# Latent attention inside a three-part block: two heads' rotated rows in one product, norm and latents in one block, first scores over three pairs of banks

## What is computed

```
kv_c = x @ W_kv;  kv_c = kv_c * rsqrt(mean(kv_c^2) + eps) * g_kv      # 32 values a token
q_c  = x @ W_q                                                         # 64 values a token
k_content, v, q_content = heads of kv_c @ W_kdec, kv_c @ W_vdec, q_c @ W_qdec   # 16 heads x 8
k_rope, q_rope = rotate(x @ W_krope), rotate(q_c @ W_qrope)            # 16 heads x 32
scores = (q . k) / sqrt(40), causal;  out = softmax(scores) @ v;  x += out @ W_o
```

## Time and profile before

| what | us |
|---|---|
| median of 3 runs | 5512.19 |
| the runs | 5452.62 to 5550.69 |
| the profiled execution, its own time | 5483.86 |
| its span (first to last instruction) | 5481.7 |
| mean granted TensorE clock over the span | 0.931 of full |

### The profile page before, as it was taken

How to read it: one execution, slowest core, us unless ns; L and a number is a source line. 1 busy time by engine, 2 the same in 40 slices (tenths; PEclk the granted TensorE clock), 3 DMA queues, 4 the chain that set the end, 5 groups by cost and what they waited for, 6 DMA issues and landing times. The chain is left out here.

```text
span 5481.7 us, 143773 instructions
## 1 busy us (share of the span) xinstructions
PE 5159.2 (94%) x46548; PEld 3167.1 (58%) x46548; DVE 3782.6 (69%) x8327; ACT 3553.5 (65%) x10714; POOL 3509.2 (64%) x4464
## 2 busy tenths in 40 slices
PE   7999999999999985899999999799999999999998
PEld 4666666666666652343434443466666666666665
DVE  5888888787887851343434444588888878888785
ACT  4888888888888850022222222488888888888885
POOL 6988888888888842000000000698888888888884
PEclk9999999999999985587978998799999999999998
DMA  2121221212212101000000000212222121221211
GB/s 73 46 60 48 55 54 45 59 49 57 52 49 60 45 24 23 0 1 1 1 1 1 1 1 1 62 46 57 51 54 57 43 60 48 56 52 45 61 47 34
DMA packets 297779, 216.59 MB, mean 40 GB/s; under 512 B 83196, under 2 KB 294680, under 8 KB 296216
## 3 DMA queue, kind: packets, MB, share of 16 engines
q1 hardware_dynamic: 296984, 206.69, 14.9%
HBM read 41.87 MB, written 1.05 MB: 8 GB/s over the span
## 5 line engine op out<-in xcount | busy, mean ns | idle before, releaser
L545 POOL TENSOR_TENSOR inv<-ssm,neg_half 128x8 f32<-128x8 f32 x768 | 1361.5, 1773 | 121.2 <-DVE ssm L864 55.9
L559 POOL TENSOR_TENSOR rot<-t 128x256 f32<-128x256 f32 x1536 | 1123.9, 751 | 334.4 <-DVE t L853 265.2
L736 ACT ACTIVATE prob<-ps,nmx,inv 128x96 f32<-128x96 f32 x3072 | 1286.1, 434 | 52.4 <-DVE nmx L850 42.9
L632 PE MATMUL ps<-w_qkv,xs 128*128 128x512 f32 x1536 | 875.0, 652 | 59.7 <-issue 30.0
L1293 ACT ACTIVATE ptl<-ps_l 128x1024 f32<-128x1024 f32 (+1 forms) x288 | 281.1, 976 | 946.6 <-PE ps_l L1168 713.4
L839 DVE TENSOR_REDUCE mx<-ps 128x4 f32<-128x384 f32 x768 | 424.9, 553 | 385.8 <-PE ps L659 382.4
L736 ACT ACTIVATION_READ_ACCUMULATOR prob<-ps,nmx,inv 128x1 f32 x3072 | 632.9, 206 | 0.0
L823 DVE TENSOR_TENSOR t<-ps,tab_s 128x256 f32<-128x256 f32 x1536 | 573.8, 413 | 37.4 <-issue 30.6
L729 ACT COPY vt<-ps 128x256 f32<-128x256 f32 x768 | 285.9, 372 | 471.5 <-PE ps L670 459.4
L831 DVE TENSOR_TENSOR prob<-prob,rec 128x384 f32<-128x384 f32 x768 | 557.6, 726 | 26.3
L720 ACT ACTIVATE sq<-ps 128x512 f32<-128x512 f32 x768 | 472.1, 615 | 112.8 <-PE ps L632 112.0
(11 more groups left out here) (201 smaller groups left out, 8641.7 us busy)
## 6 DMA issues: line engine op xcount, KB each, us to landing
vs<-vt SPq DMA_DIRECT2D x768, 96.0 KB, 2.2
vs<-vt SPq DMA_DIRECT2D x768, 64.0 KB, 2.0
vs<-vt SPq DMA_DIRECT2D x768, 32.0 KB, 1.8
xs<-x_a SPq DMA_DIRECT2D x384, 32.0 KB, 1.9
w_qkv<-in_L_ffn_Wqkv SPq DMA_DIRECT2D x48, 256.0 KB, 3.8
w_qkv<-in_L_ffn_Wqkv SPq DMA_DIRECT2D x48, 128.0 KB, 2.9
w_o<-in_L_ffn_Wo SPq DMA_DIRECT2D x12, 512.0 KB, 4.4
w<-in_L_ffn_W SPq DMA_DIRECT2D x12, 341.0 KB
```

What stands on the lines that cost most here:

```text
L545: nc.gpsimd.tensor_tensor(inv[:, n % 4], ssm[:, n % 2], neg_half[:, 0:2 * HU], ALU.pow).then_inc(z["inv_ready"], 1)
L559: nc.gpsimd.tensor_tensor(rot[:, n % 4, half[w]], t1[:, n % 2, half[w]], t2[:, n % 2, half[w]], ALU.add).then_inc(z["rotated_" + w], 1)
L632: pe.matmul(ps[:, j % 2, :], xs[:, j // UT % 2, :], w_qkv[:, 0:2, u * 256:(u + 1) * 256], start=True, stop=True).then_inc(z["qk_ready"], 1)
L736: e = nc.scalar.activation(prob[:, n % 2, h, :], scores[:, h % 2, h // 2, :], ACT.Exp, scale=inv[:, n % 4, h:h + 1], bias=nmx[:, n % 2, h: ...
```

## The change

1. **Rope.** One product a group: the weights' columns of a head are its 32 plain ones and then its 32 swapped ones, so that 128 result rows hold both heads, plain and swapped. `turn` holds cos on the plain and signed sin on the swapped rows. VectorE multiplies the 128 rows by it into ra, and, since plain and swapped rows must meet on the same partitions, makes rb in two more operations of 32 partitions, one a head. GpSimd adds 32 rows of each head, two operations. The row of ones of kT is set once. The content rows of all heads are made once (qd, kd), and SP copies a pair's rows from them into qT and kT by four DMAs a pair. ScalarE clears the row for the maxima in slot 1 of each pair.
2. **Slots.** Eight ropes at t = 0, 4, ..., 28; the turn at 4 goes to 5, the sums at 6 and 24 to 7 and 25.
3. **Norm and latents** are one block: the loads start ahead of the norm, wait for no zeroing, and the latents of group n-2 run between the norm's steps for n and n-1.
4. **Ahead of the loop** only ropes 0 and 1 come first; the others stand between the S items (EARLY), and S items take banks 4, 0 and 2 in turn.

```diff
-            pe.wait_ge(z["wl_in"], WL)
-            pe.wait_ge(z["wl_zero"], WZ)
-            for n in range(G):
...
+            for n in range(G + 2):
+                if n < G:
+                    norm_mean(nc, z, pe, nb, mean_w, q0 + n, n)
+                if 1 <= n <= G:
+                    norm_var(nc, z, pe, nb, mean_w, q0 + n - 1, n - 1)
+                if n >= 2:
+                    latents(n - 2)
+                if 1 <= n <= G:
+                    norm_spread(nc, z, pe, nb, ones_w, q0 + n - 1, n - 1)
+                if n >= 2:
+                    latent_squares(n - 2)
+                    latent_spread(n - 2)
             for n in range(G):
+                pe.matmul(ps[:, 3, :], wl_qd[:, :], qc[:, cols], start=True, stop=True).then_inc(z["qd_mm"], 1)
+                pe.matmul(ps[:, 6, :], wl_kd[:, :], kvc[:, cols], start=True, stop=True).then_inc(z["kd_mm"], 1)
...
-            def rope(pair, j, half):
+            def rope(pair, j):
+                pe.matmul(ps[:, 7, :], ws[w][:, :], src, start=True, stop=True).then_inc(z["a_ready"], 1)
...
+                bank = early_bank(y) if early else 4
+                if y == 0:
+                    pe.wait_ge(z[f"qk_rows_{b}"], 64 * (twos + 1))
+                    if not isinstance(pair, int):
+                        pe.wait_ge(z["rows_cleared"], 2 * pair)
+                if not early:
                     pe.wait_ge(z["s_read"], pair * NI + y)
+                elif y >= 3:
+                    pe.wait_ge(z["s_read"], y - 2)
...
-        TURN = {4: (0, 2), 19: (0, 3), 22: (1, 0), 29: (1, 1)}
-        SUM = {6: 0, 13: 1, 24: 2}
+        TURN = {5: (0, 2), 19: (0, 3), 22: (1, 0), 29: (1, 1)}
+        SUM = {7: 0, 13: 1, 25: 2}
+        EARLY = {0: 2, 1: 3, 2: 4, 3: 5, 10: 6, 12: 7}
...
...
+            sp.wait_ge(z["qd_copied"], G)
+            sp.wait_ge(z["kd_copied"], G)
+            for pair in range(PAIRS + 1):
+                if pair >= 2:
+                    sp.wait_ge(z["t_ready"], (pair - 1) * NI)
+                for src, dst in ((qd, qT), (kd, kT)):
+                    for h in range(2):
+                        sp.dma_start(dst[64 * h + RD + 1:64 * h + QS, pair % 2, :], src[(2 * pair + h) % HEADS * CD:((2 * pair + h) % HEADS + 1) * CD, :]).then_inc(z[f"qk_rows_{pair % 2}"], 16)
...
-                nc.gpsimd.tensor_tensor(dst[:, b, n * GT:(n + 1) * GT], ra[:, j % 2, :], rb[:, j % 2, :], ALU.add).then_inc(z["roped"], 1)
+                for h in range(2):
+                    rows = slice(64 * h, 64 * h + RD)
+                    nc.gpsimd.tensor_tensor(dst[rows, b, n * GT:(n + 1) * GT], ra[rows, j % 2, :], rb[rows, j % 2, :], ALU.add).then_inc(z["roped"], 1)
+                    pool.wait_ge(z["roped"], 2 * (pair * NR + j) + h + 1)
...
+                        if t == 1:
+                            for h in range(2):
+                                row = slice(64 * h + RD, 64 * h + RD + 1)
+                                nc.scalar.activation(qT[row, 1 - b, :], turn[row, :], ACT.Copy, scale=0.0).then_inc(z["rows_cleared"], 1)
...
+                nc.vector.tensor_tensor(ra[:, j % 2, :], ps[:, 7, :], turn[:, cols], ALU.mult).then_inc(z["ra_ready"], 1)
+                for h in range(2):
+                    swapped = slice(64 * h + RD, 64 * h + 2 * RD)
+                    nc.vector.tensor_tensor(rb[64 * h:64 * h + RD, j % 2, :], ps[swapped, 7, :], turn[swapped, cols], ALU.mult).then_inc(z["rb_ready"], 1)
```

More of the change, by code:

```diff
@@ L124, in tables @@
     e2 = np.concatenate([fr2, fr2], -1)
[L125 removed]
     sg2 = np.concatenate([-np.ones(RD // 2), np.ones(RD // 2)])
[L127 to L131, removed]
+    turn = np.concatenate([np.cos(e2).T, (np.sin(e2) * sg2).T] * 2)
+    out = dict(ident=np.eye(P), wc=wc, ws=ws, carry=carry, wmask=wmask, causal=causal, turn=turn)
     return {k: np.ascontiguousarray(v, dtype=f) for k, v in out.items()}
@@ L1012, in _ @@
         @block.gpsimd
         def _(pool):
[L1014 to L1017, removed]
+            fills = [(t[:, PAIRS:PAIRS + 2, :], 0.0) for t in wr.values()] + [(mean_kv[:, :], 1.0 / KR)]
@@ L1244, in _ @@
                         keyed(pair, b, t)
-                        if rope_at(t):
+                        if rope_at(t) is not None:
                             bank_free(t)
-                            rope(pair + 1, *rope_at(t))
+                            rope(pair + 1, rope_at(t))
                         if t in TURN:
@@ L1256, in _ @@
                         ahead, y = divmod(t + AHEAD, NI)
-                        scores(pair + ahead, b ^ ahead, y)
+                        scores(pair + ahead, b ^ ahead, y, two + (b + ahead) // 2)
                     outputs(pair, b, len(units) - 1)
@@ L1310, in _, with latent_eps @@
         def _(dve):
-            for n in range(G):
-                cols = slice(n * GT, (n + 1) * GT)
+            def latent_eps(n):
                 dve.wait_ge(z["lat_ms"], n + 1)
@@ L1380, in norm @@
                                         both[:, :, :, 0:CD], lrec[:, :, :].unsqueeze(3).to_broadcast([P, 4, 2, CD]), ALU.mult).then_inc(z["ol_normed"], 1)
-            for j in range(NR):
-                rope(0, j, "a")
-                rope(0, j, "b")
+            rope(0, 0)
+            rope(0, 1)
             for y in range(AHEAD):
+                if y in EARLY and y < 4:
+                    rope(0, EARLY[y])
                 maxima(0, y)
@@ L1388, in _ @@
                     maxima_turned(0, 0, y // 11)
+                if y in EARLY and y >= 4:
+                    rope(0, EARLY[y])
             with dve.Fori(0, PAIRS // 2) as two:
```

217 lines of the change are left out of this document (130 added, 87 removed).

## The result

| | us | ratio to before, 95% interval |
|---|---|---|
| before, beside the changed kernel | 5488.2 | |
| changed kernel, 4 runs 5250.1 to 5270.0 | 5260.5 | 0.958 (0.954 to 0.962) |
| forecast | 5355, range 5275 to 5450 | |

What follows compares the result with a forecast made beforehand. Plain loop slots were taken as bound by the TensorE-VectorE round trip, fuller slots and half clock by TensorE. 5483.9 - 60 (ahead of loop) - 81 (loop) = 5343, plus half of 28: 5357, rounded to 5355 us; range 5275 to 5450.

Steps and rivals of the forecast that it cites:

- If the same share of the work runs at half clock: Loop: 6.41 pairs at 115.5 us and 1.59 pairs at 211 us, 1076 us together, a gain of 90.
- If the same time does (373 us): Loop: 1.77 pairs at half clock in 373 us and 6.23 at 115.5, 1093 us together, a gain of 73.
- the half-clock pair: Loop at half clock: TensorE binds, 12 products of 2.00 us go, so a pair takes 211 us, not 235.
- Rival (2): Clock holds better in the loop: half-clock share falls from 0.20 to 0.10, loop 1001, kernel 5259 or 5273 us; chance 0.12.
- Rival (1): VectorE's three reads and ScalarE's clears keep the loop at 1166 us; only 60 us ahead won, 5424 or 5438; chance 0.24.
- Rival (3): Less dense TensorE holds the clock worse; at half-clock share 0.55 the loop takes 1344, kernel 5602 or 5616 us; chance 0.06.
- Blocks: Loop pair's slots at full clock, mostly in fours: summed to 115.5 us a pair, 8.2 less than before.
- The clears' 1.85 us: ScalarE's two clears a pair, 1.85 us each, 3.7 for both, making slot 3's output unit about 1 us late.
- (a): Ahead of the loop, norm, load and latents: 95.0 us becomes 71, 24 less.
- (b): Ahead of the loop, qd, kd and values up to the first rope product: 21.5 for 10.3 us, plus weights' pick, 12 more.
- (c): Ahead of the loop, first ropes: eight took 53.2 us, two are left at 11.3, 42 less.
- (d): Ahead of the loop, the 18 S items: 58.0 us becomes 52 with three pairs of banks, 6 less.

## Why the prediction was wrong, by its own steps

**The sizes were right, the share at half clock was not.** The step that failed reads "If the same share of the work runs at half clock ... If the same time does (373 us)". Neither did: the time at half clock fell from 374 to 193 us. With 115.8 us a full-clock pair, the other 811 us did 7.0 of 8 pairs, so the share fell from 0.20 to 0.125. With the forecast's own sizes and that share the loop takes 8 x (115.5 + 95.5 x 0.125) = 1020; this is 65 of the 81 us missed. The other 16 are the half-clock pair, 193 us for one pair in place of 211. Why it is shorter is not shown; no whole pair ran at half clock. The forecast priced the moved slots at full clock alone, where they give 3.2 us a pair (measured in the kernel before), and put their effect on the clock at nothing, where it is some 100 of their 124 us. Its own sign of this, a mean clock of the loop outside 0.80 to 0.90, was just met, at 0.904.

**The rivals.** Rival (2) was the right one, with its mechanism in part and its number nearly: loop 1001 forecast, 1004 measured. That the number is so near is in part luck, since its share, 0.10, was too low and its half-clock pair, 211 us, too long. It named the waits in slots 4, 6 and 24; removing them alone is worth 124 us in the kernel before (shown), of which the sums carry more than the turn (shown), while I had looked most at the turn. It had a chance of 0.12, because I held the clock to be a property of the loop as a whole, when it hangs on places in the list. It did not name the back edges, where half of the long falls lie that are left after the change. Rival (1) fell: full-clock pairs are 115 to 116 us. Rival (3), fewer products and a worse clock, is seen with the new slots alone: there the loop with 20 products a pair has a clock of 0.93, with 8 doubled 0.92, with 8 0.90. With the old slots it is the other way, 0.84 with 20 and 0.88 with 8. Each of these is one profiled execution. The Trainium skill ("TensorE: Matmul & The Clock Gate", section "A second HAM failure mode: psum-queue depth-cycling") tells of a kernel in which TensorE idles briefly between groups of products and the clock goes up and down, with no DMA to wait for; this loop agrees, with waits of 0.8 to 3.4 us ahead of its long falls.

**Full clock.** Blocks forecast 14.1, 11.6, 12.8, 25.8, 12.4, 12.3, 11.05 and 15.5 us; measured 14.3, 11.5, 12.8, 24.9, 12.6, 12.5, 11.1 and 16.1. The 0.6 us too much in the last are the 4 us at half clock in it. The clears' 1.85 us came out at 1.92. That slot 3's output unit waits for the exponential behind them is borne out: at full clock, in the kernel with two reads, TensorE stands still for 1.07 us there (3047.21). That this costs the kernel anything is not: moved to GpSimd they gave back nothing. The same duration for reads of 32 and of 128 partitions held (0.69 us), and GpSimd's two additions took 1.26 us each. The third read was charged 0.4 us in slots 0 to 3 and by the fixed 3.8 to 4.0 us of a rope slot elsewhere; a full-clock pair without it is 3 to 4 us shorter.

By the Trainium skill ("VectorE: DVE Perf Modes", section "Two Vector instructions with no wait between them") a read that starts in another quarter of the partitions than the last one does not overlap it; my estimate from it was a little over 2.1 us for three. The trace agrees: 2746.94 to 2749.10, 2.16 us.

**Ahead of the loop.** (a) 63.8 us where 71 were forecast: a middle group took 13.5 us in place of 15.8 (last spreads at 2062.64 and 2076.18), as the second spread and the squares, 2.0 and 1.8 in my list, took 1.3 and 1.05: the granted clock was 1.00 there (2059 to 2062 and 2073 to 2075), where the list had half clock throughout. The load cost 2.31 us at the first latents (3 forecast). (b) 14.6 more, 12 forecast. (c) 41.9 less, 42 forecast. (d) 6.3 less, 6 forecast; that the three pairs of banks are what makes it so is shown (79.7 us without). The sum, 64.8 against 60.

**Hidden work.** S item 0 nowhere waits for the content rows' DMAs in the trace, and GpSimd, at 176 of 1004 us, stayed hidden.

What stays open: why one short wait brings half clock and another of the same length doesn't, why a rope in slot 0 brings it at most pair ends of the changed kernel but at none of the kernel before with the new slots or of the changed one with the old slots, and what the kernel gives with all eight pairs written out, which was not run. The runs show that with the waits in the middle of pairs, the rope in slot 0 and most of the back edges gone the clock holds for a whole iteration.

## What to carry to other kernels

Where the mean clock of a loop is below 1, price a change of the order by what it does to the time at half clock, not by the wait it removes: here waits worth 3 us a pair cost 15 (124 us over eight pairs). Look in the timeline for the places where equal products double their duration, test the slots ahead of them in groups rather than one by one, and look at the loop's own back edge. When an operation is merged so that TensorE does less, count what it adds on the engine whose read releases the next scores: with the new slots, twelve products fewer won 39 us of the loop (1042 to 1004) with the third 0.69 us read and would have won 76 (to 967) without it.

## What the runs showed that I had not expected

- At each of the loop's back edges TensorE idled 2.1 to 3.4 us on issue alone, and the clock fell there, in the kernel before as in all others; between pairs within an iteration there is no such gap.
- Moving three groups of instructions by one slot changed the time at half clock in the loop from 374 to 147 us.
- Twelve products fewer a pair lowered the mean clock with the new slots (0.93 to 0.90) and raised it with the old ones (0.84 to 0.88); doubling the eight that are left raised it from 0.90 to 0.92.
